# Keys of the second cross-attention split one stage earlier, nine pooled chunks for eight, a magnitude in quarters

## The chip, the cores and the metric

The kernel runs on one core of one Trainium2 chip. Its time is the device time of one execution in microseconds (us). The engines are TensorE (PE in the rows), VectorE (DVE), ScalarE (ACT), GpSimd (POOL) and SyncE (SP), which only issues transfers. Each has its own stream of instructions, worked off in order, and waits on semaphores where it needs what another one made.

## What is computed

Two flamingo blocks on x (4 x 512 x 512) and a context ctx (4 x 1601 x 512): a gated cross-attention, a gated feed-forward, and both again in other forms. Cut to what matters:

```python
x = x + tanh(g_xattn[0]) * L0_xattn(layernorm(x), ctx, mask)   # stage A
x = x + tanh(g_ffn[0])   * L0_ffn(layernorm(x), w_up, w_down)  # stage B
x = x + tanh(g_xattn[1]) * L1_xattn(layernorm(x), ctx)         # stage C
x = x + tanh(g_ffn[1])   * L1_ffn(layernorm(x), w1, w2, w3)    # stage D
# L0_xattn: softmax(q k^T / sqrt(512)) v with one head, keys = values = ctx
# L0_ffn:   Hadamard, 8 bit per token, ternary weights, relu squared, twice
# L1_xattn: 16 heads of 32 channels; the rows are read as channels, softmax over 1601
# L1_ffn:   silu(x w1) * (x w2) w3, the weights through an NF4 round trip
```

The keys of stage C, 16 groups of 128 x 1601, are needed as a float16 part and the float16 rest of it, after a scale that comes from the largest magnitude of ctx. That magnitude, the NF4 round trip of the weights of stage D and the ternary weights of stage B are made during stage A, beside its attention.

## The kernel before

The four stages are blocks, with a barrier between them: `cross_attention_0` (A, to about 469 us of the profiled execution), `ffn_0` (B, to 701), `cross_attention_1` (C, to 1552) and `ffn_1` (D).

**Stage A** runs over K = 16 steps, k, one for each tile of 128 rows, four to a batch. TensorE makes the scores of step k in four pieces and turns the probabilities of step k - 1 between them (`turn_prob`, through two PSUM banks `a_tp`, so the third needs the first's copy), then reads out step k - 1 (26 matmuls, L706). ScalarE copies what was turned (`turned_prob`, L567 and L569; `turned_x`, L559, where a batch begins) and makes the exponentials. VectorE makes the row maximum (`maximum`, L464), adds the output two steps back (`add_out`, L498), and then does the side work of the step: after the steps 2, 6, 10 and 14 the magnitude of one batch of ctx transposed (`context_top`, L478, 128 x 6416), and from step 3 to 14 four **bites**. A bite is one level pair of the NF4 rounding of a weight piece; there are 6 pieces (n) of 8 bites (m = 0 to 7), 48 in all, and the eighth one ends with `picked`, after which `levels_ready` goes up. GpSimd's stream is in program order: `weigh(n)` waits for `levels_ready` (L358), and behind it for n > 1 stand `clip_bits(2n-4)` and `clip_bits(2n-3)` (L336, L337), on pieces of the ternary weights, then the scaling of the next weight piece. ScalarE stores the clipped bit piece m at the head of step m + 10, ahead of the copies of that step, and waits there for GpSimd:

```python
def store_bits(m):
    act.wait_ge(bit_done, m + 1)
```

The last weight piece, the last bit pieces and their stores end the stage with step 16, which only turns and reads out. SyncE loads batch b + 1 of the transposed context when `context_top(b)` has been done.

**Stage B** runs 64 units and a lag of two iterations, i. Units are (stage, batch, tile): Hadamard of x, product with w_up, Hadamard of the squares, product with w_down. ScalarE casts a high part (`copy`, L980) and moves the rounding (`move`, L989, writes `b_qm`), VectorE makes the rest (`rest`, L904), quantizes (`quantize`, L931) and scales (`scale`, L914 to L923). The scale needs the product before, the move needs the scale.

**Stage C** works off 16 slots, g, of 13 chunks of 128 keys each and four heads. TensorE makes scores of a chunk (L1533), multiplies the probabilities with the values (`c_out`, L1542), and in the 34 gaps between computes the units of the next slot's key maxima (`c_unit`, L1516, from `c_khigh`). ScalarE makes 52 exponentials a slot (L1477) into a ring of four buffers `c_prob`. The denominators come two ways: for the chunks in POOLED GpSimd adds the probabilities up (`c_prob_sum`, L1322) and TensorE does one group of eight matmuls with ones on the sum (L1561); for those in SUMMED TensorE does that group for each chunk (L1554). Beside this every slot prepares group g + 2: ScalarE scales and casts the keys (`split_keys`, L1445 and L1447), GpSimd makes the rest (`rest_of_k`, L1304), and SyncE stacks the parts of keys and queries for the next slot by 24 transfers within SBUF (L1262, L1263).

## Time and profile before

| | us |
|---|---|
| median of 3 runs | 1832.61 |
| lowest, highest | 1830.69, 1837.39 |
| the profiled execution | 1832.33 |
| its span, first to last instruction | 1830.5 |
| TensorE busy | 1610.6 |
| VectorE busy | 1184.1 |
| ScalarE busy | 841.9 |
| GpSimd busy | 826.7 |

The mean granted clock of TensorE is 0.951 of the full one. A busy share is a mean over four stages that are limited by different things, so each stage is read by itself. A wait in the timeline stands in brackets behind the work that followed it, with the engine and line that ended it.

### The profile page before, as it was taken

Reading aid. Unit: us, or ns where it says so; the run is one execution under the profiler, and the core shown is the slowest. Engines: PE = TensorE matmul, PEld = TensorE weight load, DVE = VectorE, ACT = ScalarE, POOL = GpSimd, SP = SyncE. Lnnn points to the kernel's source line nnn. Section 1 sums busy time; section 2 is a strip of 40 time slices with the busy share of each in tenths; the row PEclk is TensorE's granted clock in tenths of the full one; section 3 lists DMA queues with packets and bytes.
Section 4 is the critical chain, followed back from the end, with each engine's and each line's share of the span. In section 5 each row is a group of like instructions: output and inputs, shape, how many; then the busy total and the mean of one; then the engine's idle time right before and its main releaser. Section 6 shows DMA issues by size and latency. Waiting matters only on the chain. (4 is left out here: it accounts for less than half of the span.)

```text
span 1830.5 us, 22118 instructions
## 1 busy us (share of the span) xinstructions
PE 1610.6 (88%) x7540; PEld 614.6 (34%) x7568; DVE 1184.1 (65%) x1538; ACT 841.9 (46%) x1241; POOL 826.7 (45%) x324
## 2 busy tenths in 40 slices
PE   5999999799688886789999999899999996889898
PEld 2444444344334441122222222222222221444443
DVE  3769999887355556677767777677777641443443
ACT  1321221212334442477777777677777775111110
POOL 0022214643112222767778777687777777000000
PEclk9999999899889996799999999999999999899999
DMA  9232223023211113312222222222222241000000
GB/s 325 76 121 78 84 83 106 30 95 119 75 32 26 27 27 93 113 41 59 67 63 72 76 75 75 76 75 51 55 67 67 54 109 32 1 23 0 23 23 23
DMA packets 136395, 124.36 MB, mean 68 GB/s; under 512 B 61774, under 2 KB 112226, under 8 KB 136294
## 3 DMA queue, kind: packets, MB, share of 16 engines
q1 hardware_dynamic: 131302, 112.56, 21.7%
q10 hardware_dynamic: 4992, 10.49, 1.7%
q8 instruction: 60, 0.98, 0.2%
q14 instruction: 41, 0.34, 0.1%
HBM read 73.49 MB, written 10.76 MB: 46 GB/s over the span
## 5 line engine op out<-in xcount | busy, mean ns | idle before, releaser
L1477 ACT ACTIVATE c_prob<-c_scores,ctx_scales 128x512 f32<-128x512 f32 (+1 forms) x832 | 531.0, 684 | 221.1 <-PE c_scores L1533 218.0
L1384 DVE TENSOR_REDUCE c_piece_max<-c_unit 128x1 f32<-128x804 f32 x512 | 488.3, 987 | 208.5 <-PE c_unit L1516 205.2
L1322 POOL TENSOR_TENSOR c_prob_sum<-c_prob_sum,c_prob 128x2048 f32<-128x2048 f32 x96 | 434.8, 4529 | 90.9 <-ACT c_prob L1477 86.9
L1533 PE MATMUL c_scores<-c_queries,c_keys 97*128 97x512 f16 (+1 forms) x832 | 321.4, 392 | 40.6 <-ACT c_prob L1477 33.2
L1516 PE MATMUL c_unit<-c_khigh,c_qdiag 128*128 128x402 f16 x1024 | 274.2, 351 | 44.6 <-DVE c_piece_max L1384 32.7
L1542 PE MATMUL c_out<-c_prob,c_VT 128*32 128x512 f32 (+1 forms) x1664 | 225.0, 613 | 0.1
L1533 PEld LDWEIGHTS c_scores<-c_queries,c_keys 97*128 97x128 f16 (+1 forms) x832 | 80.9, 98 | 369.7 <-ACT c_prob L1477 322.6
L676 PE MATMUL a_S<-a_ctxT,a_xnT 128*128 128x401 f32 x512 | 190.2, 516 | 7.2 <-ACT a_prob L633 3.9
L706 PE MATMUL a_o<-a_ctx,a_probT 128*128 128x512 f32 (+1 forms) x416 | 183.2, 597 | 0.0
L1516 PEld LDWEIGHTS c_unit<-c_khigh,c_qdiag 128*128 128x128 f16 x1024 | 90.5, 100 | 152.5 <-DVE c_piece_max L1384 90.2
L567 ACT COPY a_probT<-a_tp 128x512 f32<-128x512 f32 x48 | 28.0, 585 | 217.8 <-PE a_tp L691 210.8
L1786 ACT ACTIVATE d_silu<-d_u 128x512 f32<-128x512 f32 x44 | 26.3, 597 | 212.4 <-PE d_u L1810 212.4
L676 PEld LDWEIGHTS a_S<-a_ctxT,a_xnT 128*128 128x128 f32 x512 | 95.6, 196 | 75.0 <-issue 17.1
L1739 DVE SCALAR_TENSOR_TENSOR d_hid<-d_silu,d_hscale,d_u 128x512 f32<-128x512 f32 x44 | 32.8, 746 | 120.5 <-ACT d_silu L1786 120.5
L1322 POOL TENSOR_TENSOR c_prob_sum<-c_prob 128x2048 f32<-128x2048 f32 x16 | 72.6, 4535 | 83.3 <-PE c_den L1561 75.5
L706 PEld LDWEIGHTS a_o<-a_ctx,a_probT 128*128 128x128 f32 (+1 forms) x416 | 78.7, 192 | 93.1 <-issue 93.1
L358 POOL TENSOR_TENSOR a_weights<-a_picked,a_deq 128x2816 bf16<-128x2816 bf16 x6 | 29.4, 4893 | 178.3 <-DVEq L457 178.3
L1810 PE MATMUL d_u<-d_xhi,turned_weights 128*128 128x512 f16 x352 | 94.8, 394 | 5.7 <-DVE d_xlo L1730 5.7
L1810 PE MATMUL d_u<-d_xlo,turned_weights 128*128 128x512 f16 x352 | 93.0, 388 | 0.0
L1403 DVE RECIPROCAL c_rden<-c_den 128x128 f32<-128x128 f32 x64 | 59.9, 943 | 47.7 <-PE c_den L1561 47.7
L1554 PE MATMUL c_den<-c_prob,c_ones 128*32 128x512 f32 (+1 forms) x640 | 85.9, 609 | 0.0
L450 DVE TENSOR_TENSOR a_pos<-a_pos,a_level 128x2816 bf16<-128x2816 bf16 x42 | 80.0, 1904 | 0.2
(197 smaller groups left out, 1905.8 us busy)
## 6 DMA issues: line engine op xcount, KB each, us to landing
c_k<-in_keys SPq DMA_DIRECT2D x16, 801.0 KB, 6.7
c_keys<-c_khigh SPq DMA_DIRECT2D x128, 100.1 KB, 2.2
a_ctx<-in_ctx SPq DMA_DIRECT2D x12, 1024.0 KB, 7.2
c_VT<-in_values SPq DMA_DIRECT2D x16, 768.0 KB
a_ctxT<-in_ctxT SPq DMA_DIRECT2D x12, 802.0 KB, 4.7
c_keys<-c_krest SPq DMA_DIRECT2D x64, 100.1 KB, 2.2
a_weights<-in_L_ffn_weight SPq DMA_DIRECT2D x3, 1408.0 KB, 14.4
weights_back<-a_weights SPq DMA_DIRECT2D x3, 1408.0 KB, 8.3
```

What stands on the lines that cost most here:

```text
L450: lv.did(nc.vector.tensor_tensor(pos[:], pos[:], level[1][:], ALU.max))
L676: last = nc.tensor.matmul(S4[:, n, 0:PIECE], xnT[:, d, t * P:(t + 1) * P], CT[:, d, cols], start=d == 0, stop=False)
L706: last = nc.tensor.matmul(O[k % 2][:], probT[0:w, c, :], C[0:w, c, :], start=c == 0, stop=c == MC - 1)
L1322: nc.gpsimd.tensor_tensor(psum4[:], a[:], prob[(j * MC + c) % RING][:], ALU.add).then_inc(sums_taken, 2 if i == 1 else 1)
L1384: nc.vector.tensor_reduce(piece_max[j % 2][:, k // 2, k % 2:k % 2 + 1], U[bank(unit)][:, :, 0:PIECE], axis=AX.XY, op=ALU.max).then_inc(uni ...
L1403: nc.vector.reciprocal(rden[:, cols], DEN[:, cols]).then_inc(rden_ready, 1)
L1477: nc.scalar.activation(prob[(j * MC + c) % RING][0:w, h, :], STp[h % 2][0:w, :], ACT.Exp, scale=score_scale[0:w]).then_inc(exp_done, 1)
L1516: last = nc.tensor.matmul(U[bank(unit)][:, e, 0:PIECE], QZ[o][:, h, t * P:(t + 1) * P], khigh[o][:, at:at + PIECE], start=True, stop=True)
L1533: nc.tensor.matmul(STp[h % 2][0:w, :], K[p][:, h, c * P:c * P + w], Q[p][:, h, :], start=True, stop=True).then_inc(scores_ready, 1)
L1542: last = nc.tensor.matmul(O[h * CH:(h + 1) * CH, :], VT[j % 2][0:w, c, h * CH:(h + 1) * CH], prob[(j * MC + c) % RING][0:w, h, :], start=c ...
L1554: last = nc.tensor.matmul(DEN[h * CH:(h + 1) * CH, :], ones32[0:w, :], prob[(j * MC + c) % RING][0:w, h, :], start=c == SUMMED[0], stop=False)
L1810: last = nc.tensor.matmul(U[slot(n)][:, k, :], w12T[k][:, c, f * P:(f + 1) * P], xp[part][:, c, :], start=part == 0 and c == 0, stop=part ...
```

## The change

Three things, in three stages.

**A.** `context_top` takes one quarter of one batch. The table TOPS_AT says after which maximum each runs: 0 and 1 at step 0, 2 at step 1, 3 at step 3, and for b = 1 to 3 two quarters at step 4b and two at step 4b + 1. The bites follow a table too; there are still 48. The loads of the transposed context wait for their own quarter. GpSimd's and ScalarE's code is as it was.

```diff
-        BITES_FROM, BITES_EACH = 3, 4
+        BITES_AT = {3: 4, 4: 3, 5: 4, 6: 3, 7: 4, 8: 4, 9: 4, 10: 3, 11: 4, 12: 4, 13: 4, 14: 4, 15: 3}
+        TOPS_AT = {0: [0, 1], 1: [2], 3: [3]}
+        for b in range(1, B):
+            TOPS_AT.update({4 * b: [4 * b, 4 * b + 1], 4 * b + 1: [4 * b + 2, 4 * b + 3]})
...
-                if b > 0:
-                    sp.wait_ge(ctx_topped, b)
                 for n in range(4):
                     if b > 0:
+                        sp.wait_ge(ctx_topped, (b - 1) * 4 + n + 1)
```

On VectorE in stage A, before, the end of step 8 and the maximum of step 9 (L433, L449 and L450 are a bite, L455 ends a weight piece, L464 is the maximum):

```order
L433 TENSOR_SCALAR a_level<-a_weights 128x2816 x2
L449 TENSOR_TENSOR a_neg<-a_neg,a_level 128x2816
L450 TENSOR_TENSOR a_pos<-a_pos,a_level 128x2816
L433 TENSOR_SCALAR a_level<-a_weights 128x2816
L450 TENSOR_TENSOR a_pos<-a_pos,a_level 128x2816
L455 TENSOR_TENSOR a_picked<-a_neg,a_pos 128x2816
L464 TENSOR_REDUCE a_nmax<-a_S 128x1
L465 TENSOR_SCALAR a_nbias<-a_nmax 128x1
L495 RECIPROCAL a_rinv<-a_rowsum 128x1
L496 TENSOR_SCALAR a_wout<-a_rinv,a_gv 128x1
```

The same place after, from the maximum of step 9 on (L466):

```order
L466 TENSOR_REDUCE a_nmax<-a_S 128x1
L467 TENSOR_SCALAR a_nbias<-a_nmax 128x1
L498 RECIPROCAL a_rinv<-a_rowsum 128x1
L499 TENSOR_SCALAR a_wout<-a_rinv,a_gv 128x1
L501 SCALAR_TENSOR_TENSOR x_resident<-a_o,a_wout,x_resident 128x512
L480 TENSOR_REDUCE a_ctx_tops<-a_ctxT 128x1 x2
L435 TENSOR_SCALAR a_level<-a_weights 128x2816 x2
L451 TENSOR_TENSOR a_neg<-a_neg,a_level 128x2816
L452 TENSOR_TENSOR a_pos<-a_pos,a_level 128x2816
L435 TENSOR_SCALAR a_level<-a_weights 128x2816
L452 TENSOR_TENSOR a_pos<-a_pos,a_level 128x2816
L457 TENSOR_TENSOR a_picked<-a_neg,a_pos 128x2816
```

The end of weight piece 2 stood ahead of the maximum of step 9, and now stands behind it, behind two quarters of the magnitude and one bite.

**B.** `ffn_0` gets the keys and two arrays in DRAM, `key_parts`. Group g is split in two halves of 801 columns at the iterations 4g and 4g + 2 by ScalarE, two iterations later the rests by VectorE, and at 4g + 1 ScalarE issues the stores of the group before and the load of the one after. The last group is stored, and the stores are awaited, at the end of the block. In the last batch `quantize` comes behind `scale`.

```diff
+            def store_keys(g):
+                act.wait_ge(krest_ready, 2 * g + 2)
+                for part, k in enumerate((khigh, krest)):
+                    act.dma_start(key_parts_dram[part][g], k[g % 2][:]).then_inc(k_stored[g % 2], 16)
+
+            def split_keys(g, half):
+                cols = half_of_keys(half)
+                act.wait_ge(k_loaded[g % 2], 16 * (g // 2 + 1))
+                if g > 1:
+                    act.wait_ge(k_stored[g % 2], 32 * (g // 2))
+                nc.scalar.activation(khigh[g % 2][:, cols], kt[g % 2][:, cols], ACT.Copy, scale=key_scale).then_inc(khigh_ready, 1)
...
+                nc.vector.scalar_tensor_tensor(krest[g % 2][:, cols], kt[g % 2][:, cols], key_scale, khigh[g % 2][:, cols],
+                                               ALU.mult, ALU.subtract).then_inc(krest_ready, 1)
```

On ScalarE in stage B, before, a stretch where units of both Hadamard stages alternate (L980 casts, L989 moves):

```order
L980 CAST b_ghi<-b_t 128x1024
L989 ACTIVATE b_qm<-b_y,b_magic,b_qs 128x1024
L980 CAST b_xhi<-b_t 128x512
L989 ACTIVATE b_qm<-b_y,b_magic,b_qs 128x512
L980 CAST b_ghi<-b_t 128x1024
L989 ACTIVATE b_qm<-b_y,b_magic,b_qs 128x1024
```

The same stretch after (L1041 is a half of the split, L1034 the stores, L1029 the load):

```order
L1008 CAST b_ghi<-b_t 128x1024
L1017 ACTIVATE b_qm<-b_y,b_magic,b_qs 128x1024
L1041 ACTIVATE b_khigh<-b_k,ctx_scales 128x801
L1008 CAST b_xhi<-b_t 128x512
L1017 ACTIVATE b_qm<-b_y,b_magic,b_qs 128x512
L1034 DMA key_parts<-b_khigh 128x1602
L1034 DMA key_parts<-b_krest 128x1602
L1029 DMA b_k<-in_keys 128x1602
L1008 CAST b_ghi<-b_t 128x1024
L1017 ACTIVATE b_qm<-b_y,b_magic,b_qs 128x1024
L1041 ACTIVATE b_khigh<-b_k,ctx_scales 128x801
```

In four iterations two halves and three issues are new, between a move and the next cast.

**C.** No split on ScalarE and no rest on GpSimd. `c_khigh` is loaded, the stack of the keys is filled from DRAM with all heads at once, so SyncE issues 15 stacking transfers for 24. GpSimd adds nine chunks.

```diff
-        POOLED = [0, 1, 2, 3, 5, 7, 8, 10]
+        POOLED = [0, 1, 2, 3, 5, 6, 8, 9, 11]
...
+                    for part, (k, q) in enumerate(((0, qhigh[o]), (1, qhigh[o]), (0, qrest))):
+                        rows = slice(part * CH, (part + 1) * CH)
+                        for h in range(H):
+                            sp.dma_start(Q[o][rows, h, :], q[h * CH:(h + 1) * CH, :]).then_inc(stacked, 16)
+                        src = key_parts_dram[k][bass.ds(n, 1), :, :].rearrange("o (h c) m -> c (o h) m", h=H)
+                        sp.dma_start(K[o][rows, :, :], src).then_inc(stacked, 16)
```

On ScalarE in stage C, before, one slot (L1477 are the exponentials, L1445 and L1447 the split, L1453 and L1458 the queries):

```order
L1477 ACTIVATE c_prob<-c_scores,ctx_scales 128x512 x4
L1453 ACTIVATE c_xn<-x_resident,c_nshift,c_rstd 128x512
L1458 CAST c_qhigh<-c_xn 128x512
L1477 ACTIVATE c_prob<-c_scores,ctx_scales 128x512 x4
L1445 ACTIVATE c_k<-c_k,ctx_scales 128x1602
L1447 CAST c_khigh<-c_k 128x1602
L1477 ACTIVATE c_prob<-c_scores,ctx_scales 128x512 x36
L1477 ACTIVATE c_prob<-c_scores,ctx_scales 65x512 x4
```

After (L1506, L1482 and L1487):

```order
L1506 ACTIVATE c_prob<-c_scores,ctx_scales 128x512 x4
L1482 ACTIVATE c_xn<-x_resident,c_nshift,c_rstd 128x512
L1487 CAST c_qhigh<-c_xn 128x512
L1506 ACTIVATE c_prob<-c_scores,ctx_scales 128x512 x40
L1506 ACTIVATE c_prob<-c_scores,ctx_scales 65x512 x4
```

The two instructions of the split between the second and the third chunk are gone.

## Rows read from the trace of the kernel before

**Rows 1.** Windows by stage: span, each engine's busy us, TensorE's clock, DMA share, GB/s

```profile
470.00:704.00 234.00, 181.04 (x824) 87.78 (x832) 123.46 (x305) 98.33 (x113) 45.99 (x46) 0.91 0.19 41
...
748.00:1548.00 800.00, 730.91 (x4284) 199.39 (x4284) 531.95 (x612) 597.51 (x904) 616.22 (x211) 0.98 0.26 68
```

**Rows 2.** Timeline of TensorE, first cross-attention: start us, busy us, what, wait before

```profile
266.59 11.33 PE L706 MATMUL a_o<-a_ctx,a_probT 128*128 128x512 f32 x26
...
287.92 0.66 PE L691 MATMUL a_tp<-ident,a_prob 128*128 128x128 f32 x4
...
316.68 11.33 PE L706 MATMUL a_o<-a_ctx,a_probT 128*128 128x512 f32 x26
...
342.55 1.97 PE L661 MATMUL a_tp<-ident,a_xn 128*128 128x128 f32 x8 [8.31 <-ACT a_xnT L559]
...
436.61 11.33 PE L706 MATMUL a_o<-a_ctx,a_probT 128*128 128x512 f32 x26
...
453.10 1.12 PE L691 MATMUL a_tp<-ident,a_prob 128*128 128x128 f32 x4 [4.28 <-ACT a_probT L567]
```

**Rows 3.** Timeline of VectorE, first cross-attention, steps 8 to 11

```profile
257.11 1.70 DVE L433 TENSOR_SCALAR a_level<-a_weights 128x2816 bf16<-128x2816 bf16 x2
...
262.04 0.90 DVE L433 TENSOR_SCALAR a_level<-a_weights 128x2816 bf16<-128x2816 bf16 x1
...
298.57 6.83 DVE L478 TENSOR_REDUCE a_ctx_tops<-a_ctxT 128x1 f32<-128x6416 f32 x1
...
327.72 1.83 DVE L464 TENSOR_REDUCE a_nmax<-a_S 128x1 f32<-128x1604 f32 x1
```

**Rows 4.** Timeline of GpSimd, first cross-attention

```profile
266.39 4.89 POOL L358 TENSOR_TENSOR a_weights<-a_picked,a_deq 128x2816 bf16<-128x2816 bf16 x1 [38.39 <-DVEq L457]
271.25 5.05 POOL L336 TENSOR_SCALAR a_bit<-a_bit 128x1024 f32<-128x1024 f32 x1
276.38 3.32 POOL L337 TENSOR_SCALAR a_bit_out<-a_bit 128x1024 bf16<-128x1024 f32 x1
...
440.60 4.89 POOL L358 TENSOR_TENSOR a_weights<-a_picked,a_deq 128x2816 bf16<-128x2816 bf16 x1 [36.93 <-DVEq L457]
```

**Rows 5.** Timeline of ScalarE and its queue, first cross-attention, steps 10 and 12

```profile
279.73 0.34 ACTq L590 DMA_DIRECT2D bit_weights<-a_bit_out  x1
...
281.50 0.58 ACT L567 COPY a_probT<-a_tp 128x512 f32<-128x512 f32 x1 [10.10 <-PE a_tp L691]
...
341.91 1.08 ACT L559 COPY a_xnT<-a_tp 128x512 f32<-128x512 f32 x2 [6.50 <-POOL a_bit_out L337]
```

**Rows 6.** Timeline, first feed-forward, ScalarE and VectorE in ping-pong

```profile
579.76 1.20 ACT L989 ACTIVATE b_qm<-b_y,b_magic,b_qs 128x1024 f32<-128x1024 f32 x1 [3.83 <-DVE b_qs L922]
...
585.68 1.22 DVE L904 TENSOR_TENSOR b_glo<-b_t,b_ghi 128x1024 f16<-128x1024 f32 x1 [1.75 <-ACT b_ghi L980]
...
589.48 1.20 ACT L989 ACTIVATE b_qm<-b_y,b_magic,b_qs 128x1024 f32<-128x1024 f32 x1 [3.82 <-DVE b_qs L922]
```

**Rows 7.** Instructions on the tile c_k (ns min/median/max) and its load's row

```profile
L1445 ACT ACTIVATE c_k<-c_k,ctx_scales x16: 1622/1627/1631, 707.0 to 1418.6; 128x1602 f32<-128x1602 f32 x16
L1447 ACT CAST c_khigh<-c_k x16: 1527/1527/1529, 708.6 to 1420.3; 128x1602 f16<-128x1602 f32 x16
...
c_k<-in_keys SPq DMA_DIRECT2D x16, 801.0 KB, 6.7
```

**Rows 8.** Timeline of TensorE, second cross-attention, two slots; ones-matmuls

```profile
820.50 0.39 PE L1533 MATMUL c_scores<-c_queries,c_keys 97*128 97x512 f16 x1 [1.86 <-ACT c_prob L1477]
...
869.52 0.39 PE L1533 MATMUL c_scores<-c_queries,c_keys 97*128 97x512 f16 x1 [1.86 <-ACT c_prob L1477]
...
1060.31 1.06 PE L1554 MATMUL c_den<-c_prob,c_ones 65*32 65x512 f32 x8
```

**Rows 9.** Timeline of GpSimd, second cross-attention, between slots and last slot

```profile
1063.52 4.54 POOL L1322 TENSOR_TENSOR c_prob_sum<-c_prob 128x2048 f32<-128x2048 f32 x1 [4.22 <-PE c_den L1561]
...
1534.93 9.15 POOL L1322 TENSOR_TENSOR c_prob_sum<-c_prob_sum,c_prob 128x2048 f32<-128x2048 f32 x2
```

More of the change, by code:

```diff
@@ L521, in _ @@
                     layernorm(1)
+                for i in TOPS_AT.get(k, []):
+                    context_top(i)
                 if k == 2:
@@ L534, in _ @@
                     bit_scales()
-                if k >= BITES_FROM:
-                    for _ in range(BITES_EACH):
-                        if bites:
-                            bite(*bites.pop(0))
+                for _ in range(BITES_AT.get(k, 0)):
+                    bite(*bites.pop(0))
+            assert not bites
             add_out(K - 2)
             context_scales()
-            for n, m in bites:
-                bite(n, m)
             add_out(K - 1)
@@ L772, in ffn_0 @@
         gg = [sb(f"b_gg{j}", [P, I]) for j in range(2)]
+        G, MK = keys_dram.shape[0], keys_dram.shape[2]
+        KEYS_FROM, KEY_STEPS = 0, 4
+        RESTS_FROM = KEYS_FROM + 2
+        key_scale = shared["ctx_scales"][:, 0:1]
+        kt = [sb(f"b_k{j}", [P, MK]) for j in range(2)]
+        khigh = [sb(f"b_khigh{j}", [P, MK], F16) for j in range(2)]
+        krest = [sb(f"b_krest{j}", [P, MK], F16) for j in range(2)]
         Q = 2 * B * ST
@@ L793, in ffn_0 @@
         turned = {(stage, t): sem(f"b_turned{stage}_{t}") for stage in (1, 3) for t in range(ST)}
+        k_loaded = [sem(f"b_k_loaded{j}") for j in range(2)]
+        khigh_ready = sem("b_khigh_ready")
+        krest_ready = sem("b_krest_ready")
+        k_stored = [sem(f"b_k_stored{j}") for j in range(2)]
         y_full = sem("b_y_full")
@@ L946, in _ @@
                     rest(u)
-                if pending is not None:
+                alone = v is not None and v[0] == 2 and v[1] == B - 1
+                if pending is not None and not alone:
                     quantize(pending)
@@ L951, in _ @@
                     scale(v)
+                    if pending is not None:
+                        quantize(pending)
                     pending = v
@@ L961, in _ @@
                     layernorm(u[1] + 1)
+                g, step = divmod(i - RESTS_FROM, KEY_STEPS)
+                if 0 <= g < G and step in (0, 2):
+                    rest_of_keys(g, step // 2)
             dve.wait_ge(x_added, B * ST)
@@ L1011, in _ @@
                         normalized(u[1] + 1)
+                g, step = divmod(i - KEYS_FROM, KEY_STEPS)
+                if 0 <= g < G and step in (0, 2):
+                    split_keys(g, step // 2)
+                if step == 1 and 1 <= g <= G - 1:
+                    store_keys(g - 1)
+                    if g + 1 < G:
+                        load_keys(g + 1)
+            store_keys(G - 1)
+            for j in range(2):
+                act.wait_ge(k_stored[j], 32 * G // 2)
         @block.tensor
@@ L1093, in cross_attention_1 @@
         TB = D // P
-        MK = keys_dram.shape[2]
+        MK = key_parts_dram[0].shape[2]
         PIECE = 402
@@ L1267, in slot @@
                     sp.wait_ge(stacked, (n + 1) * STACKS)
-                if nxt and (not isinstance(n, int) or n + 2 < G):
-                    load_keys(n + 2, o)
                 if more:
+                    if main:
+                        load_keys(g + 2, j % 2)
                     load_diagonal(g + 2, j % 2)
@@ L1339, in slot @@
                     return
-                add_up(g, j, 1)
-                add_up(g, j, 2)
-                add_up(g, j, 3)
-                add_up(g, j, 4)
-                add_up(g, j, 5)
-                if not isinstance(g, int) or g > 0:
-                    add_gain(g - 1)
-                add_up(g, j, 6)
-                if later:
-                    normalize(g + 3)
-                add_up(g, j, 7)
+                for i in range(1, NP):
+                    add_up(g, j, i)
+                    if i == 6 and later:
+                        normalize(g + 3)
+                    if i == 5 and (not isinstance(g, int) or g > 0):
+                        add_gain(g - 1)
                 if more:
                     rest_of_q(g + 2, j % 2)
-                    rest_of_k(g + 2, j % 2)
             every_slot(pool, slot)
@@ L1491, in slot @@
                         split_queries(g + 2, j % 2)
-                    if c == 2 and more:
-                        split_keys(g + 2, j % 2)
                 if nxt:
@@ L1885, in program @@
         if "B" in stages:
-            ffn_0(nc, shared, bit_weights, had)
+            key_parts = [nc.dram_tensor(f"key_parts{k}", list(keys.shape), F16).ap() for k in range(2)]
+            ffn_0(nc, shared, bit_weights, had, keys, key_parts)
         if "C" in stages:
@@ L1890, in program @@
             shared["turned_loaded"] = [sem(f"turned_loaded{k}") for k in range(3)]
-            cross_attention_1(nc, shared, keys, values, weights)
+            cross_attention_1(nc, shared, key_parts, values, weights)
         if "D" in stages:
```

76 lines of the change are left out of this document (30 added, 46 removed).

## The prediction, made before the changed kernel ran

> **What bounds the kernel now.** I read the windows by stage first [rows 1]. TensorE is busy 731 of the 800 us of the second cross-attention and 181 of the 234 us of the first feed-forward: it sets the time of the first, and a chain between ScalarE and VectorE leaves it 53 us idle in the second. The first cross-attention is TensorE's as well: its timeline [rows 2] shows the read-out of step 8 starting at 266.59 us, right when the scores of step 9 are done, and a step is 25.05 us where nothing waits. I call the moment at which the scores of step k are done R(k): R(9) = 266.59, R(11) = 316.68, R(15) = 436.61. A step of 25.05 is half the way from R(9) to R(11). So every us of TensorE idle in this stage is a us of the kernel, and the edits there have to be judged by the copies that TensorE waits for.
>
> **First cross-attention.** The magnitude as a whole took 6.83 us [rows 3]; quarters take a quarter each, about 1.73, and the sum is unchanged. With four bites a step it made VectorE late: the maximum of step 11 starts at 327.72, 11 us after R(11). That lateness goes, but what matters is where a weight piece ends. From the row of one bite to the next is 4.93 us, and the last bite of a piece, with picked, takes about 4.3 (262.04 to 266.4). Before, pieces 2, 3, 4, 5 ended with steps 8, 10, 12, 14. Now piece 2 ends with the second bite of step 9, and pieces 3, 4, 5 with the third bite of steps 11, 13, 15. Only then can GpSimd weigh (4.89), and then clip a bit piece in two instructions (5.05 and 3.32) [rows 4]. ScalarE issues the store of that bit piece at a fixed place of its stream, ahead of the copies of the step, and waits there. Neither GpSimd's nor ScalarE's code moves here, so the slack of before is what decides.
> Step 10: before, the store left at 279.73 and the first copy started at 281.50 only because TensorE's transposes came then [rows 5]. TensorE needs that copy at 287.92, which is R(9) + 21.3 [rows 2]. Now maximum and add_out (3.0), two quarters (3.5), one bite (4.9) and the last bite (4.3) end piece 2 at R(9) + 15.7; VectorE enters that step some 1 us late, since step 8 holds four bites and two quarters (3.0 + 3.5 + 19.7 = 26.2 against 25.05). Weighing ends at about R(9) + 21.5, clipping at + 30, and two DMA issues and the copy make it + 31. TensorE stands for 9.7 us. It restarts slowly: four transposes took 1.12 us behind the hole at 453.10 and 0.66 at 287.92, where it had been busy; for the few us of work until that is over I take 1.5. Term: **+11**.
> Step 12: here there was no slack. ScalarE's copy waited 6.50 us for the clip, and TensorE 8.31 at 342.55 [rows 2, 5]. Piece 3 ended 11.0 us after R(11); now 3.0 + 2 x 4.93 + 4.3 = 17.2. Term: **+6**.
> Step 14: piece 4 ends at R(13) + 3.0 + 3.5 + 9.9 + 4.3 + 0.4 = 21.1; weighing, clipping (7.3 to 8.4) and the copy end at + 34.7 against a need at + 21.3. Term with the restart: **+15**.
> End: piece 5 was weighed from 440.60, 4.0 us after R(15) [rows 4], and TensorE still waited 4.28 us at 453.10 [rows 2]. Now it is R(15) + 17.2, with no work of TensorE left to lay over it. Term: **+13**; this is the surest, as it has no slack in it.
> VectorE's lost lateness gives back 1 us at step 8. Sum for the stage **+44**. Low end +25 (the end, step 12, and half a stall between), high end +52 (each restart and DVE beside a busy GpSimd dearer).
> At this place VectorE and GpSimd run side by side. [Rows 4] has a clip's two instructions at 5.05 and 3.32 beside bites. The Trainium skill, page "SBUF — State Buffer", section "Who interferes with whom", says that a VectorE instruction with two SBUF inputs and a GpSimd one that reads SBUF exclude each other through the shared port. By that rule the clips would be a little dearer where bites follow a weighing and never cheaper, which speaks for this forecast's sign; no row here separates that share, and the sum leaves it out.
>
> **First feed-forward.** Added per group of keys, 16 times: on ScalarE two halves and three DMA issues, on VectorE two subtractions of 801 columns. A full-width scale took 1.627 us and a full cast 1.527 [rows 7], so a half with the type change is about 0.83. An issue on ScalarE's queue is the 0.34 of [rows 5] to 0.45; I take 0.4, so 1.2 for three. That is 2.9 us of ScalarE a group. VectorE's half is near 0.9 (half of a 1.7 us pass).
> Where the two engines play ping-pong the period of two iterations is 9.72 us [rows 6], from 579.76 to 589.48; VectorE's wait of 1.75 hides its half, but ScalarE's copy, move and copy follow one another and what is put between them lengthens the chain. A group spans four iterations. If all was in the chain: 16 x 2.9 = **46**, the upper end. If only the ping-pong stretches count (two groups a batch, three batches): 17, and with the start and the drain of the last store at the block's end (2 to 4) 20, the lower end. Between them lie the transitions, where the iterations are short, TensorE is fuller and the next keys must have landed: a load took 6.7 us [rows 7] and now stands behind two stores on the same queue. I add 4 us for each of the three and take 33: **+33**. `alone` moves one quantize of the last batch; I count it at nothing to -2, inside that.
> The Trainium skill, page "DMA: Bandwidth & Descriptors", section "Anatomy of one DMA", gives 2.0 us plus bytes over 436e3 for one DMA of GpSimd's kind, which is 3.9 us for these 801 KB, an estimate; the row has 6.7. By the page's figure keys would land in time at the transitions and the term would be nearer 21; the row decides.
>
> **Second cross-attention.** A slot is 49.02 us (820.50 to 869.52, the same hole of 1.86 us in both, [rows 8]): TensorE's scores wait while ScalarE does scale and cast of the keys, 3.16 us in the row. Without them the hole is gone: 1.86 x 13 slots and 1 us more where it was partly covered, **-25**. One group of eight ones-matmuls less in each slot, 1.06 us [rows 8]; some of it comes back as waits elsewhere, so 0.8 x 14 = **-11**. GpSimd takes the add (4.53) for the subtraction (3.22 by [rows 7]): eight adds of 4.57 (half of the 9.15 of [rows 9]) are 36.6, and with the gain, the statistics and the query's rest some 41 against a slot of now 46.4. It idled 4.22 us between slots [rows 9], and the last add keeps 2 to 4 us ahead of the matmul that reads the sum. SyncE issues 15 stacking DMAs for 24, and the key parts come from DRAM instead of from SBUF; that queue had room. In the last slot nothing else is left: its last two adds took 9.15 us without a break and ended at 1544.1, with TensorE done about then too [rows 9]; with one more, less the chunk it waits less for, the chain ends 3.5 later: **+3.5**. The start of the stage still waits for the queries' diagonals: -0.3. Sum **-34**, from -40 (whole 1.06 and the whole 3.16 of ScalarE) to -13 (only the ones-matmuls, the slot then held by GpSimd). The second feed-forward is untouched: 0.
>
> **Sum.** 1832.3 (profiled execution; the median of the runs is 1832.6, so they are one) + 44 + 33 - 34 = 1875.
>
> **Rivals.**
> 1. *ScalarE's wait bites only at step 12 and at the end.* If bites run faster than 4.9 us or GpSimd's clips are done before R(k) + 21 in steps 10 and 14, the first stage pays 19 instead of 44: 1850. For it: before, step 14 had 11 us to spare. Against: the counted finish is 9 to 13 us beyond that.
> 2. *The slack holds everywhere, and the kernel is not slower.* Place: the four store waits in the first stage. Price: all of the 44. It decides at a piece's end before R(k) + 8, so that weighing, clipping and copy (13.3 + 1) meet R(k) + 21. Then -1 there, 1832.3 - 1 + 33 - 34 = 1830. For it: VectorE is no longer late. Against: the bites stand after R(k) by the order, and no engine can start them earlier. With the feed-forward's splits hidden in the idle time of both engines as well (lower end or less, +4) it is faster: 1801.
> 3. *GpSimd becomes the bound of the second cross-attention.* An add more in each slot, ring of four buffers freed later; from a GpSimd slot over 46 us. It gives -13 in place of -34: 1896. Against: the 4.22 us idle; for: lengths on GpSimd are rough.
> 4. *The feed-forward waits for its keys each group*, 16 x 4 us: 1875 + 30 = 1905.
>
> **How the numbers follow.** Forecast 1875 with its bounds 1858 to 1893: 0.62. Rival 1 (1850): 0.12. Rival 2: 0.06 same, 0.04 faster. Rival 3: 0.11. Rival 4: 0.05. The range 1845 to 1900 leaves out rivals 2 and 4, 0.15, and some of the tails. A measurement of this kernel tells 0.5%, 9 us, from no change: faster 0.05, same 0.07, slower 0.88.
>
> **What would show it.** In the first stage: store waits of ScalarE on GpSimd of 9 to 13 us ahead of steps 10, 14 and 16 and TensorE holes as long; the maxima on time; the stage ending near 512 in place of 468. In the feed-forward: a pair of iterations of 11.75 us where the three DMA issues fall in it and of 10.55 else, a stage of 265 in place of 232. In the cross-attention: slots of 46.4, no hole at the third chunk, 816 in place of 850 us. What would make it wrong is a hole that isn't there at step 10 or 14, or a slot above 47.

## The result and the profile after

The changed kernel takes 1868.4 us (median of 4 runs, 1861.6 to 1871.2), the kernel before 1831.7 in the same comparison. The ratio is 1.019, with a 95% interval of 1.015 to 1.023: 37 us slower. The prediction was 1875, from 1845 to 1900. The profiled execution took 1870.06 us, with a span of 1868.3; head of its page (span, then busy us of each engine, share and number of instructions):

```profile
span 1868.3 us, 21928 instructions
...
PE 1596.3 (85%) x7440; PEld 613.1 (33%) x7440; DVE 1219.5 (65%) x1582; ACT 825.0 (44%) x1241; POOL 843.1 (45%) x324
```

The stages can be measured from barrier to barrier, at GpSimd's first instruction of each:

| stage | before | after | difference | forecast |
|---|---|---|---|---|
| first cross-attention (up to the barrier) | 468.9 | 517.7 | +48.8 | +44 |
| first feed-forward | 232.6 | 262.0 | +29.4 | +33 |
| second cross-attention | 851.1 | 815.6 | -35.5 | -34 |
| second feed-forward (to the span's end) | 277.9 | 273.0 | -4.9 | 0 |

Each of these is one execution. In the kernels of this study that have a stage in common, word for word, it took 258.7 to 264.5 us (first feed-forward, eight kernels) and 812.7 to 817.0 (second cross-attention, ten kernels), so a difference of a few us between two stages is not more than that spread.

The answer to [rows 2], TensorE's timeline in the first cross-attention (start, busy, what, wait before it). The rows x26 are the read-outs, which start at R(9), R(10), R(11), R(12), R(13), R(14) and R(15):

```profile
264.66 11.33 PE L706 MATMUL a_o<-a_ctx,a_probT 128*128 128x512 f32 x26
...
300.38 1.11 PE L691 MATMUL a_tp<-ident,a_prob 128*128 128x128 f32 x4 [14.32 <-ACT a_probT L567]
...
306.57 11.32 PE L706 MATMUL a_o<-a_ctx,a_probT 128*128 128x512 f32 x26
...
331.62 11.32 PE L706 MATMUL a_o<-a_ctx,a_probT 128*128 128x512 f32 x26
...
362.32 1.97 PE L661 MATMUL a_tp<-ident,a_xn 128*128 128x128 f32 x8 [18.50 <-ACT a_xnT L559]
...
381.59 11.33 PE L706 MATMUL a_o<-a_ctx,a_probT 128*128 128x512 f32 x26
...
407.02 11.32 PE L706 MATMUL a_o<-a_ctx,a_probT 128*128 128x512 f32 x26
...
442.16 1.12 PE L691 MATMUL a_tp<-ident,a_prob 128*128 128x128 f32 x4 [13.74 <-ACT a_probT L567]
...
447.44 11.33 PE L706 MATMUL a_o<-a_ctx,a_probT 128*128 128x512 f32 x26
...
472.50 11.33 PE L706 MATMUL a_o<-a_ctx,a_probT 128*128 128x512 f32 x26
...
502.17 1.12 PE L691 MATMUL a_tp<-ident,a_prob 128*128 128x128 f32 x4 [17.47 <-ACT a_probT L567]
```

From R(9) to R(10) there are 41.9 us where 25.05 would do: +16.9. From R(11) to R(12) 50.0, against 44.4 before: +5.6. From R(13) to R(14) 40.4: +15.4. From R(15) to the barrier 45.2, against 32.3: +12.9. R(9) itself comes 1.9 earlier than in [rows 2]. The sum is 48.9, the 48.8 of the table. Every one of the four holes ends with a copy of ScalarE. The waits of that stage, summed (engine, line, waited for, us in total, times, longest), say what the copies stood behind in three of the four, where before there were two waits of 7.0 and 6.5. The fourth, at step 14, is the row with "issue", which names no releaser:

```profile
ACT a_probT L567 <- POOL a_bit_out L339: 49.4, 2, 25.2
...
ACT a_probT L567 <- issue: 29.1, 1, 29.1
...
ACT a_xnT L559 <- POOL a_bit_out L339: 22.4, 1, 22.4
```

In the fourth GpSimd's clip starts at 437.71 and takes 2.77 us, the store leaves at 440.52 and the copy starts at 441.52: the same order, read from the timeline. The first of the four on ScalarE, as an answer to [rows 5]: the store leaves at 298.82 and the copy is at once behind it, after 25 us of standing:

```profile
298.82 0.34 ACTq L590 DMA_DIRECT2D bit_weights<-a_bit_out  x1
...
299.74 1.07 ACT L567 COPY a_probT<-a_tp 128x512 f32<-128x512 f32 x2 [25.16 <-POOL a_bit_out L339]
```

### The profile page after: what moved, and what is told of

The parts are those of the page before. It is cut to its first block and busy times, and to the rows that moved or that the text cites. A ratio compares the mean times of both kernels' runs of the same rounds, so it can differ in the third digit from the quotient of the medians.

```text
span 1868.3 us, 21928 instructions
## 1 busy us (share of the span) xinstructions
PE 1596.3 (85%) x7440; PEld 613.1 (33%) x7440; DVE 1219.5 (65%) x1582; ACT 825.0 (44%) x1241; POOL 843.1 (45%) x324
## 5 line engine op out<-in xcount | busy, mean ns | idle before, releaser
L1506 ACT ACTIVATE c_prob<-c_scores,ctx_scales 128x512 f32<-128x512 f32 (+1 forms) x832 | 533.7, 685 | 229.7 <-PE c_scores L1558 225.8
L1368 POOL TENSOR_TENSOR c_prob_sum<-c_prob_sum,c_prob 128x2048 f32<-128x2048 f32 x112 | 507.7, 4533 | 19.5 <-ACT c_prob L1506 11.8
L676 PE MATMUL a_S<-a_ctxT,a_xnT 128*128 128x401 f32 x512 | 194.2, 524 | 7.2 <-ACT a_prob L633 3.9
L360 POOL TENSOR_TENSOR a_weights<-a_picked,a_deq 128x2816 bf16<-128x2816 bf16 x6 | 29.4, 4894 | 263.0 <-DVEq L459 263.0
L1764 DVE SCALAR_TENSOR_TENSOR d_hid<-d_silu,d_hscale,d_u 128x512 f32<-128x512 f32 x44 | 32.8, 746 | 118.3 <-ACT d_silu L1811 118.3
L1441 DVE RECIPROCAL c_rden<-c_den 128x128 f32<-128x128 f32 x64 | 59.8, 943 | 51.7 <-PE c_den L1586 51.7
L466 DVE TENSOR_REDUCE a_nmax<-a_S 128x1 f32<-128x1604 f32 x16 | 29.2, 1825 | 94.3 <-PE a_S L679 94.3
L1116 PE MATMUL b_y<-b_had,b_ghi 128*128 128x512 f16 x128 | 55.6, 435 | 29.1 <-ACT b_qm L1017 29.1
```

The source lines that it names most:

```text
L676: last = nc.tensor.matmul(S4[:, n, 0:PIECE], xnT[:, d, t * P:(t + 1) * P], CT[:, d, cols], start=d == 0, stop=False)
L1116: last = nc.tensor.matmul(y[:, cols], gp[part][:, t, s * SPAN + c, :], had[:, c, 0:SPAN * P], start=c == 0 and part == 0, stop=c == SPAN - ...
L1368: nc.gpsimd.tensor_tensor(psum4[:], a[:], prob[(j * MC + c) % RING][:], ALU.add).then_inc(sums_taken, 2 if i == 1 else 1)
L1441: nc.vector.reciprocal(rden[:, cols], DEN[:, cols]).then_inc(rden_ready, 1)
L1506: nc.scalar.activation(prob[(j * MC + c) % RING][0:w, h, :], STp[h % 2][0:w, :], ACT.Exp, scale=score_scale[0:w]).then_inc(exp_done, 1)
```

## Why step 10 cost 17 and not 11

VectorE, an answer to [rows 3], at the end of weight piece 1 (step 7) and the maxima of steps 8 and 9:

```profile
225.90 1.62 DVE L457 TENSOR_TENSOR a_picked<-a_neg,a_pos 128x2816 bf16<-128x2816 bf16 x1
227.74 5.56 DVE L435 TENSOR_SCALAR a_neg<-a_weights 128x2816 bf16<-128x2816 bf16 x1 [0.22 <-DVE a_picked L457]
233.22 5.59 DVE L435 TENSOR_SCALAR a_pos<-a_weights 128x2816 bf16<-128x2816 bf16 x1
...
243.66 1.82 DVE L466 TENSOR_REDUCE a_nmax<-a_S 128x1 f32<-128x1604 f32 x1
...
269.73 1.82 DVE L466 TENSOR_REDUCE a_nmax<-a_S 128x1 f32<-128x1604 f32 x1
...
291.05 1.72 DVE L435 TENSOR_SCALAR a_pos<-a_weights 128x2816 bf16<-128x2816 bf16 x1
```

GpSimd at the same places, an answer to [rows 4]:

```profile
227.66 4.90 POOL L360 TENSOR_TENSOR a_weights<-a_picked,a_deq 128x2816 bf16<-128x2816 bf16 x1 [25.04 <-DVEq L459]
232.51 5.56 POOL L356 TENSOR_TENSOR a_weights<-a_weights,a_srecip 128x2816 bf16<-128x2816 bf16 x1
...
285.48 4.89 POOL L360 TENSOR_TENSOR a_weights<-a_picked,a_deq 128x2816 bf16<-128x2816 bf16 x1 [47.42 <-DVEq L459]
```

`picked` ends piece 1 at 227.5 and GpSimd starts to weigh it. The next bite stands right behind, and its first two picks take 5.56 and 5.59 us, where a pick took 0.90 in [rows 3]. Each ends 0.7 us behind the end of a GpSimd instruction: 233.3 behind the weighing's 232.6, and 238.8 behind the scaling's 238.1. VectorE waits there for the whole of GpSimd's instruction. Together the two take 9.4 us more than two picks of 0.90. In the kernel before, the end of piece 1 had one such pick and not two, because the maximum stood behind `picked`; it stood beside GpSimd's scaling, which started at 223.09:

```profile
223.27 5.47 DVE L433 TENSOR_SCALAR a_neg<-a_weights 128x2816 bf16<-128x2816 bf16 x1
```

So step 7 ran over, and the maximum of step 8 starts 4.4 us after R(8) (243.66 against 239.23). It was 3.1 late there before (244.24 against 241.15), but step 8 held no quarters then and made it up. Now step 8 has four bites and two quarters, 26.1 us from maximum to maximum, and passes the lateness on: the maximum of step 9 starts at 269.73, 5.1 us after R(9). My sum had VectorE on time at step 8 and counted 1. Without the 9.4 us of the two picks it would have been on time (an estimate from these rows). Piece 2 then ends as counted, 15.6 us after that start, and weighing and clipping take 13.3. That makes 4.1 of the 5.9 us; the restart cost 2.6 (16.9 less the hole of 14.3) where I took 1.5.

The Trainium skill has this in "SBUF — State Buffer", section "Who interferes with whom": an instruction of VectorE in a mode that uses both ports and one of GpSimd exclude each other, and the loser blocks for the other's whole instruction. The rows agree for the weighing and the scaling. For a clip they do not: the pick at 291.05 starts 0.7 us into a clip of 5.04 us and takes 1.72, not the rest of it, while that clip is longer than the next one of its kind, 3.63 with VectorE idle. In the prediction I had asked of the page only what GpSimd would lose, and not what VectorE would, though the trace of before has the pick of 5.47 us. That no work lay between the two is read from the rows; no kernel here changed it alone.

## The first cross-attention by experiments

The first four kernels are the changed one with one piece put back or moved. All comparisons are with the kernel before on the same chip.

**a_both_old: both tables as before.**

```diff
-        BITES_AT = {3: 4, 4: 3, 5: 4, 6: 3, 7: 4, 8: 4, 9: 4, 10: 3, 11: 4, 12: 4, 13: 4, 14: 4, 15: 3}
-        TOPS_AT = {0: [0, 1], 1: [2], 3: [3]}
-        for b in range(1, B):
-            TOPS_AT.update({4 * b: [4 * b, 4 * b + 1], 4 * b + 1: [4 * b + 2, 4 * b + 3]})
+        BITES_AT = {k: 4 for k in range(3, 15)}
+        TOPS_AT = {4 * b + 2: [4 * b, 4 * b + 1, 4 * b + 2, 4 * b + 3] for b in range(B)}
```

> The changed kernel with the first cross-attention's side work as before: four bites in each of the steps 3 to 14, and all four quarters of the magnitude in a row at the steps 2, 6, 10, 14. Theory (the first stage costs 49 us through the stores that ScalarE waits for): the stage ends near 469 us again, no wait of ScalarE on GpSimd above 7 us in it, and the kernel comes to 1868 - 49 = 1819 us, below the kernel before by the 35 of the second cross-attention less the 29 of the feed-forward. Rival (the key work in the feed-forward, or the transfers, disturb more than that and the first stage is only a part): 1835 to 1850.

Measured: 1819.7 us, ratio 0.995 (0.992 to 0.997), the stage 469.0. The 49 us lie in the tables, and the other two parts together are worth 11 us.

**a_bites_old: the bites as before, the quarters as changed.**

```diff
-        BITES_AT = {3: 4, 4: 3, 5: 4, 6: 3, 7: 4, 8: 4, 9: 4, 10: 3, 11: 4, 12: 4, 13: 4, 14: 4, 15: 3}
+        BITES_AT = {k: 4 for k in range(3, 15)}
```

> The changed kernel with the bites as before (four in each of the steps 3 to 14), the magnitude's quarters left where the change puts them. Theory: the bites carry the loss, the quarters carry none, so the first stage is at 469 us or up to 10 below, since VectorE is late no more at steps 7 and 11; the kernel 1810 to 1819 us. Rival (the quarters at steps 8, 9, 12, 13 push the bites over the edge of their steps): the stage above 480, the kernel above 1830.

Measured: 1806.1 us, ratio 0.987 (0.982 to 0.991), the stage 454.5, and 456.2 to 456.9 in the three kernels below that have the same first stage. The quarters are worth 12 to 14 us; I had put 0 to 10 on them. Against a_both_old 4.0 us lie between R(11) and R(12), where VectorE's maximum of step 11 is 6.9 us late and not 11, and 6.6 behind R(15), where a hole of 4.5 us at step 16 is gone. In the steps from 5 on one hole above 1 us is left; its row on TensorE:

```profile
334.56 1.97 PE L661 MATMUL a_tp<-ident,a_xn 128*128 128x128 f32 x8 [8.91 <-ACT a_xnT L559]
```

**a_tops_old: the magnitude as before, the bites as changed.**

```diff
-        TOPS_AT = {0: [0, 1], 1: [2], 3: [3]}
-        for b in range(1, B):
-            TOPS_AT.update({4 * b: [4 * b, 4 * b + 1], 4 * b + 1: [4 * b + 2, 4 * b + 3]})
+        TOPS_AT = {4 * b + 2: [4 * b, 4 * b + 1, 4 * b + 2, 4 * b + 3] for b in range(B)}
```

> The changed kernel with the magnitude as before (four quarters in a row at the steps 2, 6, 10, 14) and the bites by the new table. Theory (bites alone): the end of the pieces stays behind the maxima of steps 9, 11, 13, 15. At step 9 and 13 no quarter stands ahead of the piece's end any more (3.5 us earlier), so the stalls at steps 10 and 14 shrink by 3 us each, those at 12 and 16 stay: stage near 512 us, kernel 1860 to 1866. Rival (quarters): the stage returns below 480, kernel below 1830.

Measured: 1868.2 us, ratio 1.020 (1.017 to 1.023), the stage 516.0, 2 and 4 us above what I had said. TensorE's four holes:

```profile
296.11 1.12 PE L689 MATMUL a_tp<-ident,a_prob 128*128 128x128 f32 x4 [9.82 <-ACT a_probT L565]
...
360.22 1.97 PE L659 MATMUL a_tp<-ident,a_xn 128*128 128x128 f32 x8 [21.33 <-ACT a_xnT L557]
...
435.71 1.12 PE L689 MATMUL a_tp<-ident,a_prob 128*128 128x128 f32 x4 [9.44 <-ACT a_probT L565]
...
500.81 1.12 PE L689 MATMUL a_tp<-ident,a_prob 128*128 128x128 f32 x4 [22.15 <-ACT a_probT L565]
```

The stalls of steps 10 and 14 went from 14.3 and 13.7 to 9.8 and 9.4 (I had said 3 less each). Those of steps 12 and 16 grew by 3 and 5, which fits the magnitude standing in steps 10 and 14 again, ahead of the pieces that end in 11 and 15; I had said they would stay. The verdict does not hang on that: with the bites' table the loss is there in either form, without it in none.

**a_store_late: the tables as changed, ScalarE's stores at the end of a step.**

```diff
-                if 2 <= m:
-                    store_bits(m - 2)
...
+                if 2 <= m:
+                    store_bits(m - 2)
+                if 2 <= m < len(bits):
+                    act.wait_ge(bit_done, m - 1)
+                    load_bits(m + len(bits))
                 if 0 <= m < len(bits):
                     scale_bits(m)
```

> The changed kernel with the new tables as they are, and only ScalarE's store of the clipped bits and the load behind it moved from the head of a step to its end, behind the exponentials. Theory (a wait placed ahead of the copies, nothing else): the holes of 14, 18, 14 and 17 us at steps 10, 12, 14 and 16 are gone, the stage ends where GpSimd's last clip and its store end, some 37 us after the scores of step 15, near 462 us; kernel 1810 to 1818. Rival (VectorE itself is late and holds the exponentials): the holes move to the exponentials and the kernel stays above 1840.

Measured: 1825.3 us, ratio 0.996 (0.995 to 0.998), the stage 472.5. The holes of 14 to 18 us are gone, with no bite moved, so the place of the wait is what made late bites expensive (the load behind the store moved with it). But the stage ended 10 us later than I had said, and the kernel 7 us above my range. Its rows (ScalarE and its queue around one load; GpSimd's last clip):

```profile
437.29 0.48 ACTq L579 DMA_DIRECT2D a_bit<-in_L_ffn_w_down  x1
...
441.19 1.24 ACT L600 ACTIVATE a_bit<-a_bit,a_magic,a_bit_recip 128x1024 f32<-128x1024 f32 x1 [2.64 <-DMA a_bit<-in_L_ffn_w_down]
...
467.09 2.77 POOL L339 TENSOR_SCALAR a_bit_out<-a_bit 128x1024 bf16<-128x1024 f32 x1
```

The scaling of a bit piece now stands directly behind the load that it needs, and waits for it in six steps, 16.3 us in all, ahead of the next copies; and the last clip ends at 469.9, from where only its store is left. That is GpSimd's chain behind the last bite, the end term of the prediction: from R(15) to the barrier there are 44.8 us here, 45.2 in the changed kernel and 32.3 before.

**ab_old_and_late: bites as before and stores at the end of a step.**

Its edit is that of a_bites_old and that of a_store_late together.

> Base as before (a_bites_old, 1806 us, first stage 454.5 us, with one hole of 8.91 at step 12). ScalarE's stores of the clipped bits are moved to the end of the steps as in a_store_late. Theory: the hole at step 12 shrinks to under 2 us, the end is GpSimd's no more but TensorE's: stage 443 to 447, kernel 1794 to 1799. Rival (the later store delays the next load and with it GpSimd's clips and the last store): stage at 454 or above, nothing gained.

Measured: 1799.5 us, ratio 0.982 (0.981 to 0.984), the stage 452.0, 2.5 below a_bites_old where I had said 8 to 11. The hole at step 12 was 3.5 in place of 8.9; 1.1 of it is the scaling's wait for the load, which stands ahead of that copy. From R(11) to R(12) the kernel is 4.6 us shorter. Behind R(15) nothing changed (25.8 us in both), and a_bites_old comes to R(9) 2.1 us earlier, ahead of all the moved stores; the other kernels with the old bites come there as late as this one. So the miss is a gain that I put too high and a base that came out 2 us low.

**late_copies_only: tables as changed, stores between the copies and the exponentials.** There the load has the exponentials' time to land.

```diff
-                if 2 <= m:
-                    store_bits(m - 2)
...
                     for n in range(4):
                         turned_prob(k - 1, n)
+                if 2 <= m:
+                    store_bits(m - 2)
+                if 2 <= m < len(bits):
+                    act.wait_ge(bit_done, m - 1)
+                    load_bits(m + len(bits))
                 if k < K:
                     act.wait_ge(max_ready, k + 1)
```

> The changed kernel with its own tables, and only ScalarE's stores of the clipped bits between the copies of a step and its exponentials. Theory: the copies wait no more; what is left in the stage is VectorE's lateness after a bite that meets GpSimd's weighing (5.6 us for a pick that takes 0.9 alone), and the end, where GpSimd's last clip and store come 40 us after the scores of step 15: stage 465 to 472 us, kernel 1817 to 1825. Rival (the wait only moves to the exponentials, which then hold the next step's turns): above 1830.

Measured: 1825.8 us, ratio 0.997 (0.995 to 0.998), the stage 473.3, just outside what I had said for both, and the same as a_store_late: with pieces that end this late it is the exponentials that wait for the store (a hole of 5.2 us at 418.3). With the new table some 20 us (472.5 against the 452.0 of ab_old_and_late) came back in neither of the two orders tried.

## The first feed-forward by experiments

An answer to [rows 6], ScalarE in the changed kernel over one period with the transfers and the half period before it:

```profile
639.27 1.20 ACT L1017 ACTIVATE b_qm<-b_y,b_magic,b_qs 128x1024 f32<-128x1024 f32 x1 [3.83 <-DVE b_qs L936]
640.37 0.95 ACT L1041 ACTIVATE b_khigh<-b_k,ctx_scales 128x801 f16<-128x801 f32 x1
...
644.33 0.34 ACTq L1034 DMA_DIRECT2D key_parts<-b_khigh  x1
644.71 0.45 ACTq L1034 DMA_DIRECT2D key_parts<-b_krest  x1
645.19 0.92 ACTq L1029 DMA_DIRECT2D b_k<-in_keys  x1
646.21 1.01 ACT L1008 CAST b_ghi<-b_t 128x1024 f16<-128x1024 f32 x1 [1.10 <-PE b_t L1083]
651.04 1.20 ACT L1017 ACTIVATE b_qm<-b_y,b_magic,b_qs 128x1024 f32<-128x1024 f32 x1 [3.82 <-DVE b_qs L936]
```

From move to move of 1024 columns it is now 11.77 us (639.27 to 651.04), and 10.57 where only a half stands in it (628.70 to 639.27), against 9.72. I had written 11.75 and 10.55. The half at 640.37 takes 0.95 us, and the three issues stand between the move and `b_ghi`. VectorE's halves are 1.05 us and are hidden where it waited.

**b_transfers_alone.** From here on the base is a_bites_old, whose feed-forward takes 260.7 us. This kernel leaves out the halves from the third group on, so most of its key parts are not the keys'; the waits of its loads and stores are changed to fit (not shown).

```diff
-                if 0 <= g < G and step in (0, 2):
+                if 0 <= g < 2 and step in (0, 2):
                     split_keys(g, step // 2)
...
-                if 0 <= g < G and step in (0, 2):
+                if 0 <= g < 2 and step in (0, 2):
                     rest_of_keys(g, step // 2)
```

> Base: the kernel with the bites as before and the new quarters (a_bites_old, 1806 us, feed-forward 260.7 us from barrier to barrier). Left out: from the third group of keys on, ScalarE's halves and VectorE's halves; the stores and loads stay with their 1.2 us on ScalarE's queue, so most of the key parts aren't the keys'. Theory (ScalarE's chain carries all of the 28 us): 28 halves of 0.85 are gone and the transfers' 1.2 x 14 stay, so the feed-forward comes down by 10 to 20 us, to 241 to 251. Rival 1 (the transfers' issue and their traffic are the whole cost): it stays above 256. Rival 2 (they cost nothing, the halves are all): 233.

Measured: the feed-forward 244.1 us (kernel 1787.2): the halves are worth 16.6 of the 28 us, the transfers 11.5. With the halves ScalarE's waits for the loads of the keys are gone too, 11.4 us in four waits in the base. TensorE stood 3.6 us behind the longest of them and under 1 behind each other one, so some of the 16.6 may be the landing of the loads and not the halves' own time.

**b_issues_on_sync.**

```diff
...
+            todo = [(at[stage - 1, b, t] + 3, 0, (stage, b, t)) for stage, b, t in units if stage in (1, 3)]
+            todo += [(KEY_STEPS * g + 1, 1, g) for g in range(1, G)]
+            for _, kind, what in sorted(todo):
+                if kind == 1:
+                    store_keys(what - 1)
+                    if what + 1 < G:
+                        load_keys(what + 1)
+                    continue
...
-                if step == 1 and 1 <= g <= G - 1:
-                    store_keys(g - 1)
-                    if g + 1 < G:
-                        load_keys(g + 1)
```

> Base as before (a_bites_old, 1806 us, feed-forward 260.7). The stores and the loads of the keys are issued by SyncE, between its transposes, in place of ScalarE; all else is as in the base. Theory (ScalarE's time in the chain): 15 times 1.2 us go from ScalarE, of which the ping-pong stretches (half the groups or a little more) give back 8 to 14 us: feed-forward 247 to 253, kernel 1793 to 1799. Rival (SyncE's waits for the rests hold up the transposes behind them, or landing decides): 260 or more.

Measured: 1793.2 us, ratio 0.978 (0.977 to 0.980), the feed-forward 248.2: 12.5 us less, inside what I had said. ScalarE now goes from move to cast without a gap (no row of its queue between):

```profile
575.30 1.20 ACT L1034 ACTIVATE b_qm<-b_y,b_magic,b_qs 128x1024 f32<-128x1024 f32 x1 [3.83 <-DVE b_qs L953]
576.41 0.95 ACT L1053 ACTIVATE b_khigh<-b_k,ctx_scales 128x801 f16<-128x801 f32 x1
...
580.37 0.78 ACT L1034 ACTIVATE b_qm<-b_y,b_magic,b_qs 128x512 f32<-128x512 f32 x1 [2.53 <-DVE b_qs L949]
581.04 1.00 ACT L1025 CAST b_ghi<-b_t 128x1024 f16<-128x1024 f32 x1
```

The period is 10.56 in both halves of a group. 12.5 is all that the transfers cost by the run before it, within the spread of such a stage, so they cost by their issue in ScalarE's stream. What is left over the kernel before is 15.6 us, no more than the 16.6 that went with the halves, so the traffic (26.2 MB more in and out) shows no cost beyond ScalarE's waits for three loads, 7.8 us in all, with 1.2 us of TensorE idle behind the last. The two, 16.6 and 12.5, make up the 28 to within 1 us.

## The second cross-attention by experiments

TensorE's ones-matmul on GpSimd's sum, one slot apart, and in the last slot, as answers to [rows 8] and [rows 9]:

```profile
938.31 1.06 PE L1586 MATMUL c_den<-c_prob_sum,c_ones 128*32 128x512 f32 x8
...
984.62 1.06 PE L1586 MATMUL c_den<-c_prob_sum,c_ones 128*32 128x512 f32 x8
...
1586.68 1.94 PE L1586 MATMUL c_den<-c_prob_sum,c_ones 128*32 128x512 f32 x8 [3.30 <-POOL c_prob_sum L1368]
```

A slot is 46.31 us (46.4 was forecast), and in the last one TensorE waits 3.30 us for GpSimd's last add (3.5 was forecast).

**c_eight_pooled.**

```diff
-        POOLED = [0, 1, 2, 3, 5, 6, 8, 9, 11]
+        POOLED = [0, 1, 2, 3, 5, 7, 8, 10]
```

> Base as before (a_bites_old, 1806 us, second cross-attention 813.3 us from barrier to barrier, 851.1 before the change). GpSimd adds eight chunks as before the change, TensorE has its ones-matmuls for five. Theory (the sum was 25 us by the removed split, 11 by the ones-matmuls less 3.5 in the last slot): a slot of 47.2 against 46.4, and no wait in the last one: second cross-attention 820 to 822, kernel 1813 to 1815. Rival (GpSimd's ninth add costs the slots what it saves, and the split is the whole gain): 813, kernel 1806 or lower.

Measured: 1811.9 us, ratio 0.989 (0.987 to 0.991), the stage 817.8, 1 and 2 us below what I had said. Its slot:

```profile
921.80 1.06 PE L1586 MATMUL c_den<-c_prob_sum,c_ones 128*32 128x512 f32 x8
...
968.88 1.07 PE L1586 MATMUL c_den<-c_prob_sum,c_ones 128*32 128x512 f32 x8
```

47.08 against 46.31 is what I had taken, 0.8. Over the stage the ninth chunk brings 4.5 us and not 7.5: some slots differ by less, and the last one is 2.5 longer. Even of the 4.5, 2.2 lie in the seventh slot, which took 50.0 to 52.1 us in kernels with the same stage, so it is worth 1 to 5. The removed split is then worth 851.1 - 817.8 = 33.3, to some 2 us, against the 25 that I gave it. Why is in the trace of before, which I had not read far enough. I took the slot from two holes that were 49.02 apart. From one ones-matmul on the sum to the next there are fifteen distances, of which six are 50.1 to 50.7 and one 53.0 (that one is long after the change as well, 51.7). Two slots of before, behind the hole of 1.86 us (eight matmuls with the values in each; then the windows of the two slots, with the granted clock as the third number from the right):

```profile
870.42 1.06 PE L1542 MATMUL c_out<-c_prob,c_VT 128*32 128x512 f32 x8
...
918.54 0.39 PE L1533 MATMUL c_scores<-c_queries,c_keys 97*128 97x512 f16 x1 [1.86 <-ACT c_prob L1477]
...
919.71 1.94 PE L1542 MATMUL c_out<-c_prob,c_VT 128*32 128x512 f32 x8
```

```profile
861.00:910.00 49.00, 45.29 (x274) 12.62 (x272) 35.41 (x41) 37.54 (x58) 39.30 (x14) 1.00 0.27 70
911.00:960.00 49.00, 45.30 (x265) 12.37 (x262) 34.51 (x41) 36.58 (x56) 39.27 (x14) 0.97 0.24 66
```

The same hole, but in the second slot TensorE comes back at the lower of its two clocks: eight matmuls take 1.94 us in place of 1.06, and that slot is 1.6 us longer. So the hole cost 1.9 or 3.5 us, whichever it was; 13 holes of 1.86 and six times 1.6 are 33.8, which fits the 33.3. What decides between the two prices no run shows. With the split away the hole is gone, and no slot of the changed kernel but the seventh is above 47.2.

**split_in_place and best_try: is the move worth it?** Both have the bites as before, the quarters, and the stores between copies and exponentials. The first leaves keys and pooled chunks as they were before the change; the second has them as changed, with the transfers issued by SyncE.

> The kernel before with the quarters and the stores between copies and exponentials, but with the keys split in the second cross-attention and eight pooled chunks, as before. It asks whether the moved split is worth its place. From the measured parts: first stage 443 (469 before), all else as before: 1831 - 26 = 1805 us; best_try is to be 22 to 26 below it (second cross-attention -36 to -38, feed-forward +16). Rival (the move pays only because of something else it brought): best_try not below this one.

> Bites as before, quarters of the magnitude, SyncE issues the transfers of the keys, and ScalarE's stores of the clipped bits stand between the copies of a step and its exponentials (not behind the exponentials, where the load that follows had to be waited for, 2.7 us in each of six steps). From the measured parts: 1793.2 (issues on SyncE) less the hole of 8.91 and its slow restart at step 12. Theory: first stage 442 to 446 us in place of 454 to 456, kernel 1780 to 1785. Rival (the first stage is then held by GpSimd's chain at its end): 1790 or more.

Measured: split_in_place 1807.1 us, ratio 0.987 (0.985 to 0.990). best_try 1784.8 us, ratio 0.975 (0.972 to 0.977), 2.5% faster than before and the fastest of all. The one hole above 2 us that is left in the first stage from step 5 on:

```profile
330.10 1.97 PE L661 MATMUL a_tp<-ident,a_xn 128*128 128x128 f32 x8 [2.29 <-ACT a_xnT L559]
```

The moved split with nine chunks and SyncE's issues is worth 22.3 us. The first stage of best_try is 449.9, not 442 to 446. The hole at step 12 is 2.3, so 6.6 of the 8.9 us came back, and R(11) to R(12) is 6.8 us shorter than in a_bites_old. Behind R(15) the 25.8 us are unchanged. I had counted on the whole hole and its restart.

## Why the prediction was right

- **Step 10, +11: mis-sized, +16.9.** The failed part is VectorE's lateness, 1 us in my sum and 5.1 in the trace: the sum had it on time at step 8, and two picks behind GpSimd's weighing and scaling had made it 4.4 us late. The restart was 2.6 and not 1.5. Cause read from the rows, not isolated. "The maxima on time" was a sign that failed.
- **Step 12, +6: right**, +5.6. **Step 14, +15: right**, +15.4. **End, +13: right**, +12.9, and by a_store_late the only term that doesn't hang on ScalarE's order. The earlier VectorE gave 1.9 and not 1.
- **The mechanism of the stage is shown**: putting the bites back takes all of it away (a_both_old, a_bites_old), putting the magnitude back takes nothing (a_tops_old), and moving only the wait takes 45 us (a_store_late, which also takes most of the hole that step 12 had before). Rival 1 (only step 12 and end) and rival 2 (slack holds) fall with the four holes. They are 13.7 to 18.5 us long, where I had named 9 to 13 for the steps 10, 14 and 16.
- **Feed-forward, +33: a little too large**, +29.4. The two periods were right to 0.02 us. ScalarE waited for a load of keys three times, 10.1 us in all, in the place that I had given 12, but TensorE was idle for only 3.3 us behind the three. Rival 4 falls.
- **Second cross-attention, -34: right in the sum, -35.5, by two errors that met.** The split was worth 33 and not 25 (the clock behind the hole), the ninth chunk 4.5 and not 7.5. That they met is luck. The terms as written also add up to -32.8 and not to -34. Rival 3 falls: GpSimd still idles 4.65 us between slots, where it idled 4.22 before.
- **The total, +43: +38 in the spans.** The stages are off by +5, -4, -1 and -5 us. Part of that cancels, so the total is nearer than its terms, which is luck too.
- **Second feed-forward, 0: -4.9.** Its granted clock is 1.00 over three stretches of 40 us in which it was 0.96 before, with the same instructions. It was 272.3 to 273.3 us in every kernel of this study whose second cross-attention has no split, and 275.0 in split_in_place. What of the work before it decides that clock stays open. One stretch of it before and after (160 us behind the barrier in both):

```profile
1712.60:1752.60 40.00, 39.42 (x173) 17.65 (x177) 14.10 (x24) 4.18 (x7) 0.00 (x0) 0.96 0.00 0
```

```profile
1755.30:1795.30 40.00, 40.00 (x187) 18.14 (x186) 13.50 (x22) 4.18 (x7) 0.00 (x0) 1.00 0.00 0
```

## What to carry to other kernels

Side work is not free because its engine has time left: look at who reads its last piece and where in that reader's stream the wait stands. A wait for slack work belongs behind everything that the critical engine will ask of the same stream, and the transfer behind it needs its landing time before its first use. Count the holes of a loop over all its rounds, not over the two that happen to be on the screen.

## What I had not expected of the hardware

- A pick of VectorE that takes 0.90 us alone took 5.56 us when GpSimd's 4.89 us instruction had started 0.1 us before it, and 2.45 when it came 3.2 us into it. It waits for the end of GpSimd's weighing or scaling, and adds its own time; beside a clip it took 1.72.
- One idle stretch of 1.86 us on TensorE had two prices, with or without about 3 us at half the clock behind it (0.97 in place of 1.00 over 49 us).
- An added 26.2 MB of transfers in 262 us, which took the DMA share from 0.18 to 0.47, cost little or nothing that could be seen once ScalarE did not issue it (248.2 us at a share of 0.49).
